# An attention stage with three mixings: the first mixing spread over two steps, projections moved, the output addition on another engine, iterations written out

## The reference, cut to what matters

```
scores = q @ k.T * scale + q . rel_k[i - j]          # 16 heads of 64, 512 x 512 each, per batch
threshold = the 32nd largest score of each row       # kernel: TOPK = 512 // 4 // 4
attn = softmax(scores where >= threshold, else -inf)
v1 = attn @ v + sum_j attn[i, j] * rel_v[i - j]      # mixing 1
v2 = attn @ v1                                       # mixing 2
v3 = attn @ v2                                       # mixing 3
res = alpha1 * v1 + alpha2 * v2 + alpha3 * v3
x = x + res @ Wout.T + bout
```

## Time and profile before

| | |
|---|---|
| median of 3 runs | 3139.66 us |
| profiled execution | 3144.04 us (span 3142.3 us) |
| attention's steps on VectorE | first MAX8 at 64.4 us, last step ends at 2421 us |
| everything after attention | from about 2466 us |
| busy, whole span | PE 2607.6, DVE 2719.1, POOL 2163.7, ACT 2027.7 us |

### The profile page before, as it was taken

How to read it: one execution, slowest core, us unless ns; L and a number is a source line. 1 busy time by engine, 2 the same in 40 slices (tenths; PEclk the granted TensorE clock), 3 DMA queues, 4 the chain that set the end, 5 groups by cost and what they waited for, 6 DMA issues and landing times. The chain is left out here.

```text
span 3142.3 us, 66621 instructions
## 1 busy us (share of the span) xinstructions
PE 2607.6 (83%) x15200; PEld 1498.6 (48%) x15200; DVE 2719.1 (87%) x6639; ACT 2027.7 (65%) x6207; POOL 2163.7 (69%) x2732
## 2 busy tenths in 40 slices
PE   4788888888788888888888888888888685988857
PEld 2444444444444444444444444444444444777743
DVE  5999999999999999999999999999998374765646
ACT  2677777877777777777777777777787152222214
POOL 1788888888888888888888888888888142221105
PEclk7899999999999999999999999999999696776659
DMA  4444444444444444444444444444443000000001
GB/s 119 118 132 134 129 127 125 129 132 125 131 126 129 127 127 127 128 126 130 131 129 126 130 125 134 125 125 131 127 131 100 4 29 14 8 6 1 0 8 48
DMA packets 401017, 318.44 MB, mean 101 GB/s; under 512 B 33246, under 2 KB 388648, under 8 KB 400808
## 3 DMA queue, kind: packets, MB, share of 16 engines
q1 hardware_dynamic: 398660, 314.18, 34.7%
q10 hardware_dynamic: 2148, 2.33, 0.3%
HBM read 139.48 MB, written 136.58 MB: 88 GB/s over the span
## 5 line engine op out<-in xcount | busy, mean ns | idle before, releaser
L870 DVE MAX8 top<-work 128x8 f32<-128x512 f32 x1536 | 980.7, 681 | 0.0
L880 DVE MATCH_REPLACE8 work<-top,work 128x512 f32<-128x512 f32 x1024 | 685.5, 678 | 0.0
L949 POOL TENSOR_TENSOR scores<-scores,cut 128x512 f32<-128x512 f32 x512 | 643.7, 1279 | 0.0
L562 PE MATMUL bank<-probs_t,u 128*64 128x512 f32 x2048 | 467.7, 598 | 1.4 <-ACT u L760 1.4
L794 ACT ACTIVATE probs_of_tile<-scores,minus_max_and_least 128x512 f32<-128x512 f32 x512 | 373.9, 748 | 89.7 <-POOL scores L949 89.2
L959 POOL TENSOR_SCALAR probs_of_tile<-probs_of_tile,inverse 128x512 f32<-128x512 f32 x512 | 349.0, 692 | 84.1 <-DVE inverse L845 61.4
L867 DVE MAX8 top<-scores 128x8 f32<-128x512 f32 x512 | 325.9, 679 | 82.8 <-issue 63.5
L940 POOL TENSOR_SCALAR cut<-scores,minus_max_and_least 128x512 f32<-128x512 f32 x512 | 354.2, 692 | 62.7 <-issue 39.5
L880 DVE MATCH_REPLACE8 work<-top,scores 128x512 f32<-128x512 f32 x512 | 342.7, 678 | 0.0
L771 ACT ACTIVATE probs_t<-bank 128x512 f32<-128x512 f32 x512 | 283.6, 609 | 66.7 <-PE bank L646 66.5
L945 POOL TENSOR_SCALAR cut<-cut 128x512 f32<-128x512 f32 x512 | 305.8, 613 | 21.5
(11 more groups left out here) (251 smaller groups left out, 5062.7 us busy)
## 6 DMA issues: line engine op xcount, KB each, us to landing
probs_scratch<-probs_of_tile SPq DMA_DIRECT2D x256, 256.0 KB, 2.5
band<-probs_scratch SPq DMA_DIRECT2D x256, 256.0 KB, 3.2
rel_scratch<-rel SPq DMA_DIRECT2D x256, 254.0 KB, 3.1
relj<-rel_scratch SPq DMA_DIRECT2D x256, 128.0 KB, 2.3
relj<-rel_scratch SPq DMA_DIRECT2D x512, 64.0 KB, 2.5
xt<-stream_normed_t SPq DMA_DIRECT2D x64, 256.0 KB, 2.4
pair_j<-table_j SPq DMA_DIRECT2D x64, 193.5 KB, 2.2
pair_o<-table_o SPq DMA_DIRECT2D x64, 66.0 KB, 1.9
```

Of the source, the lines that this page charges most:

```text
L562: last = nc.tensor.matmul(U[HEADS[h], :], lhs, pt[mpar][:, h, jt, :], start=(jt == 0), stop=(jt == NT - 1 and step > 0))
L870: nc.vector.max(top[q][:, h, 8 * r:8 * r + 8], work[:, h, :]).then_inc(s.next_tops, 1)
L880: nc.vector.match_replace(out=work[:, h, :], in_to_replace=top[q][:, h, 8 * r:8 * r + 8], in_values=sc[Tc][:, h, :] if r == 0 else work[:, ...
L949: nc.gpsimd.tensor_tensor(sc[Tc][:, h, :], sc[Tc][:, h, :], cut[:, h, :], ALU.add).then_inc(s.masked, 1)
```

## The change: what it does

1. `run_iterations` writes out every iteration (8 batches of 8, then 3 to drain). No loop, no register values: `Slots` holds plain numbers.
2. The staging copies `pj`, `po`, `xt` and their semaphores go; TensorE, ScalarE and GpSimd read the tables `t.TJ`, `t.TO` and `k.XNT` where they lie.
3. The first mixing is split by columns: at T = 1 the first 384 of 512 columns and the band's first 256; at T = 2 the last 128 and the band's last 256.
4. Projections move: K from T = 0 of its own iteration to T = 1 of the one before; Q from T = 3 to T = 2 of the one before; V from T = 1 to T = 2, behind the mixing. ScalarE's copies move with them (V's to the head of T = 3, behind L722), and the waits for the bank `MISC` are set anew.
5. The output: VectorE's L851 goes. ScalarE copies the bank to a new tile `outs` at T = 2, GpSimd adds it to the stream at the head of its T = 2.
6. ScalarE's copy of the turned band (L804) goes ahead of the exponentials.

```
-    with eng.Fori(first // 2, last // 2) as g:
-        for par in range(2):
-            for T in range(NT):
-                body(Slots(g, par, T), par)
+    for g in range(B):
+        batch(g)
+    batch(B, 3)
...
-                if T == 2 and (it := z.iteration(1)) is not None:
...
-                    sp.dma_start(pj[1 - par][:, :], t.TJf[:, bass.ds(at_pair, J_COLS)]).then_inc(s.pj_in[1 - par], 16)
-                    sp.dma_start(xt[1 - par][:, :], t.XNT[:, bass.ds(at_batch, N)]).then_inc(s.pj_in[1 - par], 16)
...
+                if T == 1 and av is not None:
+                    pe.wait_ge(s.probs_kept, (av * NT + 3) * 2)
+                    pe.wait_ge(s.v_kept, av + 1)
+                    mix(av, par, 0, 0, 3 * P)
+                    pe.wait_ge(s.band_kept, av * NT + 2)
+                    mix_band(0, 2 * P)
                 if T == 2 and av is not None:
-                    pe.wait_ge(s.probs_kept, (av + 1) * 2 * NT)
-                    pe.wait_ge(s.v_kept, av + 1)
-                    mix(av, par, 0)
+                    pe.wait_ge(s.probs_kept, (av + 1) * NT * 2)
+                    mix(av, par, 0, 3 * P, N)
                     pe.wait_ge(s.band_kept, (av + 1) * NT)
...
+                    mix_band(2 * P, N).then_inc(s.mixed, 1)
+                if T == 2 and prev is not None:
+                    if nxt is not None:
+                        pe.wait_ge(s.q_kept, nxt + 1)
...
+                                                k.XNT[:, tokens(prev, jt * P, (jt + 1) * P)],
+                                                t.TJ[:, z.pair(-1), J_WV:J_WV + P], start=True, stop=True)
+                    last.then_inc(s.v_made, 1)
...
+                if T == 2 and old is not None:
+                    act.wait_ge(s.out_made, old + 1)
+                    if not early(old):
+                        act.wait_ge(s.out_added, old)
+                    nc.scalar.activation(outs[:, :], MISC[:, :], ACT.Copy).then_inc(s.out_kept, 1)
...
-                        nc.vector.tensor_tensor(Xb, MISC[:, :], Xb, ALU.add).then_inc(s.out_added, 1)
...
+                if z.T == 2 and (old := z.iteration(-3)) is not None:
+                    pool.wait_ge(s.out_kept, old + 1)
...
+                    nc.gpsimd.tensor_tensor(Xb, outs[:, :], Xb, ALU.add).then_inc(s.out_added, 1)
```

More of the change, by code:

```diff
@@ L466, in mixing @@
         if T == 3 and av is not None:
-            return av, 1, par
+            return av, 1, par, z.pair(-2)
         if T < 2 and old is not None:
-            return old, T + 2, 1 - par
+            return old, T + 2, 1 - par, z.pair(-3)
         return None
@@ L553, in body, with mix @@
                 cur, nxt = z.iteration(0), z.iteration(1)
-                def mix(it, mpar, step):
-                    if not early(it * ORDER + step):
+                def mix(it, mpar, step, lo=0, hi=N):
+                    if lo == 0 and not early(it * ORDER + step):
                         pe.wait_ge(s.mixed_kept, it * ORDER + step)
@@ L561, in mix, with mix_band @@
                             lhs = v[mpar][:, jt, HEADS[h]] if step == 0 else u[:, jt, h, :]
-                            last = nc.tensor.matmul(U[HEADS[h], :], lhs, pt[mpar][:, h, jt, :],
-                                                    start=(jt == 0), stop=(jt == NT - 1 and step > 0))
+                            last = nc.tensor.matmul(U[HEADS[h], lo:hi], lhs, pt[mpar][:, h, jt, lo:hi],
+                                                    start=(jt == 0 and lo == 0), stop=(jt == NT - 1 and step > 0))
+                    return last
+                def mix_band(lo, hi):
+                    for h in range(2):
+                        last = nc.tensor.matmul(U[HEADS[h], lo:hi], t.relv[:, :], bt[par][:, h, lo:hi],
+                                                start=False, stop=(hi == N))
                     return last
@@ L610, in body @@
                 if m and m[1] < 3:
-                    it, step, mpar = m
+                    it, step, mpar, _ = m
                     pe.wait_ge(s.mixed_kept, it * ORDER + step)
[L613 to L617, removed]
+                    if T == 0:
+                        pe.wait_ge(s.u_kept, it * 2 + 1)
+                    elif prev is not None:
                         pe.wait_ge(s.v_kept, prev + 1)
+                    elif old is not None:
+                        pe.wait_ge(s.out_kept, old + 1)
                     for jt in range(NT):
@@ L649, in body @@
                         last.then_inc(s.probs_turned, 1)
[L651 to L656, removed]
-                                     start=True, stop=True).then_inc(s.k_made, 1)
[L658 to L672, removed]
+                if T == 1 and nxt is not None:
+                    if old is not None:
+                        pe.wait_ge(s.u_kept, old * 2 + 2)
+                    elif av is not None:
+                        pe.wait_ge(s.v_kept, av + 1)
+                    elif cur is not None:
+                        pe.wait_ge(s.q_kept, cur + 1)
+                    nc.tensor.matmul(MISC[:, :], t.TJ[:, z.pair(1), J_WK:J_WK + P], k.XNT[:, tokens(nxt)],
+                                     start=True, stop=True).then_inc(s.k_made, 1)
                 e = z.back(7)
@@ L834, in body @@
             def body(z, par):
-                T = z.T
-                old = z.iteration(-3)
                 def aside():
```

129 lines of the change are left out of this document (62 added, 67 removed).

## The result

The changed kernel takes 3028.0 us (median of 4 runs, 3018.7 to 3034.1), the kernel before 3136.6 beside it on the same chip: a ratio of 0.965, 95% interval 0.962 to 0.968. Predicted were 3032 and the range 3022 to 3086. The profiled execution took 3031.7 us.

What follows compares the result with a forecast made beforehand. VectorE was taken to bound the kernel: 3144.0 - 75.5 (pass starts) - 37.2 (addition off VectorE) + 0.8 (start) - 0.7 (end) = 3031.4, told as 3032 us. Range 3022 to 3086.

Steps and rivals of the forecast that it cites:

- the start and the end: Around the attention: +0.8 us (0 to +2) at the first projections, -0.7 us (-3 to +2) after the last mask.
- Pass starts, -75.5: VectorE's loop: 29 pass starts of 2.6 us each go when iterations are written out, 75.5 us, straight code costing nothing.
- Rival B: VectorE's gaps stay, code fetch stalling as often in straight code: 3107 us; chance 0.06.
- L851, -37.2: Output addition leaves VectorE: 62 additions of 0.60 us off its path, 37.2 us, with ScalarE and GpSimd not binding.
- The first mixing, +0.2 to +1.3: TensorE's split: T = 1 gains about 3.3 us, T = 2 loses 3.2; the total grows by 0.2 to 1.3.
- The relay's sum of 34.0: TensorE and ScalarE passing one bank, projections moved: 34.0 us an iteration against 35.06, so VectorE still sets the pace.
- The range's upper bound: The TensorE-ScalarE relay takes 35.9 us an iteration if the matmuls around it run at 1.2 GHz for a stretch: 3086.
- rival C: TensorE's wait for Q's copy lowers its clock, T = 3's mixing takes 7.3 us: 3198, slower than before; chance 0.05.
- 34.1 us an iteration: GpSimd's work with the output addition: 34.1 us against VectorE's 35.06, so GpSimd does not bind.
- the pattern forecast: GpSimd falls behind VectorE by 0.26 us twice; half is made good at T = 2, the rest at T = 3.
- V's wait: TensorE's V projection waits for Q's copy, the last thing in ScalarE's T = 2: 0.5 to 1 us.
- A: The relay becomes the bound and VectorE waits for scores: 3086 at 35.9 us an iteration, typical 3054; chance 0.14.

Runs made afterwards that it cites:

- e3: Kernel before with only VectorE's loop cut to passes of one iteration, 58 instead of 29: 3069.8 us, ratio 0.981.
- e1: Kernel before with every engine's loop written out, nothing else changed: 3091.5 us, ratio 0.989.
- e2: Kernel before with VectorE's stream alone written out, the other engines keeping their loop: 3078.0 us, ratio 0.983.
- e9: Changed kernel with the output addition back on VectorE, without ScalarE's copy and GpSimd's addition: 3061.1 us, ratio 0.975.
- e4: Kernel before with only the output's addition moved, ScalarE copying and GpSimd adding: 3140.8 us, ratio 1.002.
- e7: Changed kernel with the split taken out, the first mixing whole at T = 2: 3261.1 us, ratio 1.043.
- e6: Kernel before with all loops written out, addition moved and first mixing split; projections and staging as before: 3021.3 us, ratio 0.965.
- e5: Kernel before with all loops written out and the output's addition moved to ScalarE and GpSimd, no split: 3143.9 us, ratio 1.003.
- e8: e5 with sixteen transposes of the identity in TensorE's wait at T = 2: 3132.9 us, ratio 1.000.
- e8's repetition: Same kernel as e8, meant to have 28 transposes but run with sixteen: 3136.7 us, ratio 0.999.
- e10: Changed kernel with two more 128x512 scalings on GpSimd at T = 2, written to tiles nothing reads: 3034.8 us, ratio 0.967.

## Why the prediction was right, and where its working was not

**Size.** Predicted 3031.4 in the profiled execution's terms, 3031.7 measured. Attention's last addition ended at 2353.2 us instead of 2465.5, 112.3 earlier; the sum had 112.6. So close a hit is luck in part. The 255 steps took 2236.9 us (predicted 2235.1), 110.3 less than before; the rest came from the start and the end, where the sum had 0.1 in all: the first step began 0.2 us earlier and not 0.8 later, and the end took 1.8 us less. What follows attention happened to take the same in both profiled executions, 676.8 and 676.9 us, where it scatters by 18 us over all of them.

**Pass starts, -75.5.** Right in the changed kernel: no idle time without a releaser is left. In the trace of the kernel before the gaps are 28, of 2.1 to 3.3 us, some 72 in all (three of them are put down to ScalarE's scores there); the term held some 4 us of other things. e3 shows that they go with the length of the pass; that a fetch fills them is not shown. Rival B is out. But the term is not a property of the loop alone: e1 gave 42 us, e2 and e3, which change VectorE's stream only, 56 and 64. In e1 VectorE waits for the others instead, which is what the prediction named ("at these gaps the other engines also caught up") and left without a price.

**L851, -37.2.** Right in the changed kernel by e9 (33 in the times, 35 at attention's end). Without the split it is 0 in e4 and a loss of some 50 us on top of e1: VectorE has 0.60 us less to do at each T = 2, but waits for scores take its place and more.

**The first mixing, +0.2 to +1.3.** The quarter takes 1.09 us, estimate 1.1, three quarters 2.80, estimate 2.75. The step that fell short is how this edit was read: as a rearrangement with a small cost of its own, in a relay said to be about 34 us. Without it the other two terms do not add up; it is what makes their sum real. Undone (e7) the kernel is slower than before by 4%; added alone on top of the two (e6) it brings 123 us. The relay's sum of 34.0 was for the split order; there it stayed under VectorE's 35.07, and whether it is 34.0 no run shows. Nor would the same sum have warned: made for the order without the split, where T = 1 gets shorter by what T = 2 gets longer, it gives nearly the same (the rival of e7, 3028 to 3040 us), and e7 took 3261. It adds the four steps up and has no term for a single step that is too long, nor for a wait that one order has and the other hasn't.

**The clock.** The range's upper bound (35.9, "if the matmuls around it run at 1.2 GHz for a stretch") and rival C had the mechanism, but sought it in the changed kernel, at T = 3. It acts at T = 2 in the kernels without the split: TensorE idles 3.5 us behind ScalarE's copies of the transposed probabilities, and the mixing behind that takes 5.35 us (C had priced a slow one at 7.3). In the changed kernel the wait there is 1.1 to 2.2 us, mostly about 1.4, and what follows it is a quarter of the mixing; 3 of its 128 pieces of the first mixing and 4 of its 128 second and third mixings ran slow. In e5, e8 and e8's repetition VectorE's late steps come almost only behind slow mixings; this is a correlation within each run, since nothing set the clock on purpose. In e7 VectorE waits behind fast mixings too. So the split removes two things, the exposure to a low clock and the sheer length of TensorE's T = 2, and how its 123 us divide between them stays open. That holding the clock up by other means restores the gain isn't shown either: in e8 idle time was left behind the filler, and neither a longer filler nor one of plain matmuls in place of transposes was run.

**GpSimd.** 34.1 us an iteration stands, by e10. Its lag behind VectorE in the changed kernel (0.15, 0.42, 0.69, 0.18 us at T = 3, 0, 1 and 2) is the pattern forecast, twice 0.26 and then made good at T = 2; the idle time left is about 1 us at T = 3, where 0.5 was forecast. Its addition took 1.27 us and waited for ScalarE's copy 7 times in 64, 14.1 us in all.

**Relay, V's wait.** V's projection waits 0.46 us for Q's copy, under the 0.5 to 1 given, and VectorE's waits for scores after the first step are 0.7 us in all: A didn't come.

## What to carry to other kernels

When one engine is at its limit and gaps are taken from it, check the relay of the others at the new pace step by step and not only in sum over the iteration (the sum of e7's order came out under 35.06 and was wrong by over 200 us in the whole), and run the parts of the change one on top of the other; in a tight pipeline they don't add up, and the one that looks like mere rearrangement can carry the rest (here, added in turn, the loop's end gained 42 us, the addition's move lost some 50, and the split gained 123). Where a stall of TensorE is followed by its longest piece of work, look at the granted clock there: in e5 the stall was paid for twice, once as idle time and once in the matmuls behind it. The mean clock alone does not tell: 0.98 in e6 cost nothing, and 0.94, 0.96 and 0.95 went with 3136, 3092 and 3144 us (the kernel before, e1, e5). A small deficit of an engine with buffers ahead of it is not to be multiplied by all iterations: it costs only from where the lead is used up (e10).

## What the runs showed of the hardware

- Behind waits of 1.8 us and more TensorE's granted clock often fell: the next sixteen 128x512 matmuls, or most of them, ran at 1.2 GHz, a mean of 0.68 to 0.69 in two windows, 5.35 us for 3.65. It is not certain: in the repetition of e8, behind waits of 1.55 to 2.36 us they were fast in 15 iterations, behind waits of 1.80 to 3.08 slow in 45; the ranges overlap, so the length of the wait alone doesn't decide. In the changed kernel waits of mostly 0.5 to 1.9 us and at most 2.3, four to five an iteration, went with 0.997 over 1900 us, with three falls.
- Passes of about 365 instructions cost VectorE 2.1 to 3.3 us at 28 of their starts, passes of about 180 instructions nothing that can be seen, with twice as many of them.
- On GpSimd a scalar comparison of 128x512 takes 2.00 us where multiply, add, min and max take 0.61 to 0.70; a power of 128x2 takes 0.73.
- VectorE's recorded durations can drift while its pace does not: MAX8 goes from 0.69 us early to 0.73 late in the changed kernel, with steps at 8.77 us throughout, and stays at 0.69 in e1, whose code is written out as well. Read its cost from starts.
